# Alternating the heads of the mixer's mix, and conditioning units on Vector and Scalar alone

## The reference

```
def bi_wkv(r, k, v, w, u, time_emb):                   # the conditioning unit; k = v = f, a side input
    tf    = sigmoid(sum(time_emb))
    decay = exp(-exp(w)) * (0.5 + 0.5 * tf)            # one value per (batch, channel)
    ek, ekv = exp(min(k, 30)), exp(min(k, 30)) * v
    nf, df  = forward  scans  a = a * decay + ekv,  b = b * decay + ek
    nb, db  = backward scans of the same
    euk = exp(min(u + k, 30))
    num = nf + nb - ekv + euk * v
    den = df + db - ek  + euk
    return sigmoid(r) * num / max(den, 1e-8) * (0.8 + 0.2 * tf)

x = x + mamba2_mixer(bi_wkv(x, f, f, ...))             # 32 heads of 64, state 128, conv of 4 taps
x = x + moe0(bi_wkv(x, f, f, ...))
x = x + latent_attention(bi_wkv(x, f, f, ...))
x = x + gqa_and_moe1(bi_wkv(x, f, f, ...))
```

## Time and profile before

| | us |
|---|---|
| median of 3 runs | 1410.94 |
| lowest and highest run | 1410.77 to 1413.26 |
| the profiled execution | 1404.55 |
| its span | 1402.80 |
| TensorE busy | 1195.4 (85%) |
| VectorE busy | 850.6 (61%) |
| ScalarE busy | 581.1 (41%) |
| GpSimd busy | 568.0 (40%) |

### The profile page before, as it was taken

How to read it: one execution, slowest core, us unless ns; L and a number is a source line. 1 busy time by engine, 2 the same in 40 slices (tenths; PEclk the granted TensorE clock), 3 DMA queues, 4 the chain that set the end, 5 groups by cost and what they waited for, 6 DMA issues and landing times. The chain is left out here.

```text
span 1402.8 us, 16347 instructions
## 1 busy us (share of the span) xinstructions
PE 1195.4 (85%) x4614; PEld 644.4 (46%) x4614; DVE 850.6 (61%) x1244; ACT 581.1 (41%) x1710; POOL 568.0 (40%) x531
## 2 busy tenths in 40 slices
PE   0059999699995999999968989888898888988998
PEld 0024554355543444444434646443783437844443
DVE  7979996699964752364248749369541695414232
ACT  2025555365542322232226646567571675701110
POOL 5574876248763310020026749357540475400000
PEclk9999999999997999999989999989899898997999
DMA  6000000000034000000030000030000000000000
GB/s 260 0 22 1 1 1 1 1 0 0 0 124 162 0 0 0 0 0 0 34 150 1 1 0 0 17 126 1 1 2 1 1 1 0 1 8 0 0 0 30
DMA packets 5485, 33.28 MB, mean 24 GB/s; under 512 B 528, under 2 KB 1936, under 8 KB 3536
## 3 DMA queue, kind: packets, MB, share of 16 engines
q1 hardware_dynamic: 5424, 32.61, 6.0%
HBM read 31.56 MB, written 1.05 MB: 23 GB/s over the span
## 5 line engine op out<-in xcount | busy, mean ns | idle before, releaser
L806 POOL TENSOR_TENSOR decays<-decays,scores 128x768 f32<-128x768 f32 x64 | 122.6, 1920 | 117.5 <-ACT decays L742 117.2
L575 PE MATMUL pg<-h,weights 128*128 (+1 forms) x136 | 67.5, 621 | 78.0 <-PEq L356 76.7
L1991 POOL TENSOR_TENSOR f_pair<-m,weights 128x256 f32<-128x256 f32 x80 | 91.0, 1156 | 95.4 <-DVE m L2012 94.3
L1094 PE MATMUL ph<-h,weights 128*128 x256 | 115.8, 597 | 0.0
L1399 POOL TENSOR_TENSOR prob_latent<-prob_latent,inverse_latent 128x128 f32<-128x128 f32 (+1 forms) x128 | 81.5, 660 | 70.1 <-DVE inverse_latent L1389 69.7
L742 ACT ACTIVATE decays<-pcum,neg_cum 128x256 f32<-128x256 f32 (+1 forms) x256 | 86.3, 426 | 9.9 <-PE pcum L628 9.6
L1239 DVE TENSOR_TENSOR mid<-up,ph 128x512 f32<-128x512 f32 x44 | 30.2, 687 | 98.5 <-ACT up L1151 98.5
L1399 POOL TENSOR_TENSOR prob_gqa<-prob_gqa,inverse_gqa 128x128 f32<-128x128 f32 (+1 forms) x128 | 62.1, 506 | 58.3 <-DVE inverse_gqa L1389 56.5
L879 DVE SCALAR_TENSOR_TENSOR conv<-px,pp,conv 128x510 f32<-128x510 f32 (+2 forms) x102 | 75.9, 744 | 15.9 <-ACT conv L714 13.5
L1151 ACT ACTIVATE up<-ph 128x512 f32<-128x512 f32 x44 | 26.3, 597 | 140.5 <-PE ph L1094 140.5
L575 PE MATMUL px<-h,weights 128*128 x136 | 70.5, 643 | 14.0 <-DVE conv L879 14.0
(11 more groups left out here) (326 smaller groups left out, 2981.7 us busy)
## 6 DMA issues: line engine op xcount, KB each, us to landing
weights<-in_w_mixer SPq DMA_DIRECT2D x2, 2048.0 KB, 18.4
weights<-in_w_moe SPq DMA_DIRECT2D x2, 1536.0 KB, 8.0
moe_rest<-in_w_moe SPq DMA_DIRECT2D x2, 1536.0 KB, 13.5
weights<-in_w_gqa SPq DMA_DIRECT2D x1, 3072.0 KB, 10.2
weights<-in_w_gqa SPq DMA_DIRECT2D x1, 2048.0 KB, 14.6
weights<-in_w_moe SPq DMA_DIRECT2D x1, 1920.0 KB, 8.7
weights<-in_w_mixer SPq DMA_DIRECT2D x1, 1536.0 KB, 12.6
weights<-in_w_moe SPq DMA_DIRECT2D x1, 1152.0 KB, 12.0
```

Of the source, the lines that this page charges most:

```text
L575: op = nc.tensor.matmul(out[0:m, :], w[:, col + k * m:col + (k + 1) * m], net.h[:, ds(i * PAIR + k * TOK, TOK)], start=(k == 0), stop=(k = ...
L806: nc.gpsimd.tensor_tensor(decays[:, head % 4], decays[:, head % 4], scores[:], ALU.mult).then_inc(decay_scaled, 1)
L1094: op = nc.tensor.matmul(out[:], wt[:, n * D + k * P:n * D + (k + 1) * P], net.h[:, ds(i * PAIR + k * TOK, TOK)], start=(k == 0), stop=(k = ...
L1991: op = nc.gpsimd.tensor_tensor(out[:, :, s, :], src[:, :, 1 - s, :], sin[:, None, s, :].to_broadcast([P, 4, HALF]), ALU.mult)
```

## The change

In `mix`, the loop over the two heads becomes the innermost one: the matmul calls alternate between head 0 and head 1, behind one wait for both heads' decays. The same 16 instructions are issued.

In `CondUnit`, GpSimd's eight operations per unit go. ScalarE gets the four decay spreads (one per channel half and batch entry, a copy of ones with a scale column, 128 x 256) and the copy of e (128 x 1028) as `scalar_operands`; its copy of f goes. VectorE gets e x f, own, own x f, num += num_b and num += ev_pair, two halves each, so that its list has 36 steps and not 26. The waits on GpSimd's semaphores become waits on ScalarE's (`decay_spread`, `e_copied`) and on VectorE's own earlier steps. The operands are issued on ScalarE in the condition stage ahead of each pair's exponential, in the mixer behind the first two convolution starts and ahead of the softplus exponential, in the first MoE stage behind the silu of tile 1, and in latent attention at step 1. The diff, cut:

```diff
-    VECTOR_LINKS = 7 * KT
+    VECTOR_LINKS = 12 * KT + 1
...
-    def pool_operands(self, pair, turn):
...
-    def pool_numerator(self, turn):
...
+    def scalar_operands(self, pair, turn):
         net, nc = self.net, self.net.nc
+        nc.scalar.wait_ge(self.factor_made, turn)
         for kt in range(KT):
+            for b in range(BB):
+                at = (kt * BB + b) * SEG
+                col = net.dcol[:, ds((self.c * KT + kt) * BATCH + pair * BB + b, 1)]
+                nc.scalar.activation(net.decay[:, at + 1:at + SEG],
+                                     net.ones[:, 0:1].to_broadcast([P, SEQ]), ACT.Copy,
+                                     scale=col).then_inc(self.decay_spread, 1)
+        nc.scalar.activation(net.e_pair[:], net.e[:, ds(pair * UNIT, UNIT)], ACT.Copy) \
+            .then_inc(self.e_copied, 1)
+
+    def scalar_exp(self, turn):
         net, nc = self.net, self.net.nc
         nc.scalar.wait_ge(self.u_ready, turn + 1)
         nc.scalar.activation(net.euk[:], net.euk[:], ACT.Exp).then_inc(self.euk_ready, 1)
-        nc.scalar.activation(net.f_pair[:], net.f[:, ds(pair * UNIT, UNIT)], ACT.Copy) \
-            .then_inc(self.f_copied, 1)
...
+        def e_times_f(k):
+            here, both = columns(k)
+            ev_done[k] = link.mark(v.tensor_tensor(net.ev_pair[:, here], net.e[:, both],
+                                                   net.f[:, both], ALU.mult))
...
-                v.wait_ge(self.operand_ready, 4 * turn + operands)
+                v.wait_ge(self.decay_spread, KT * BB * turn + (k + 1) * BB)
+                if x is net.ev_pair:
+                    v.wait_ge(*ev_done[k])
+                if x is net.e_pair:
+                    v.wait_ge(self.e_copied, turn + 1)
...
+        def own(k):
+            here, both = columns(k)
+            v.wait_ge(self.euk_ready, turn + 1)
+            own_done[k] = link.mark(v.tensor_tensor(net.euk[:, here], net.euk[:, here],
+                                                    net.e[:, both], ALU.subtract))
+
+        def own_times_f(k):
+            here, both = columns(k)
+            v.wait_ge(*own_done[k])
+            v.wait_ge(*num_b_done[k])
+            ev_done[k] = link.mark(v.tensor_tensor(net.ev_pair[:, here], net.euk[:, here],
+                                                   net.f[:, both], ALU.mult))
...
         stages = [
-            add_u,
-            scan(net.den, net.e, 2), scan(net.num, net.ev_pair, 3),
-            scan(net.num_b, net.ev_pair, 3, True), scan(net.den_b, net.e_pair, 4, True),
-            combine(net.den, net.den_b), add_own, bound,
+            add_u, e_times_f,
+            scan(net.den, net.e, den_done), scan(net.num, net.ev_pair, num_done), own,
+            scan(net.num_b, net.ev_pair, num_b_done, True),
+            scan(net.den_b, net.e_pair, den_b_done, True),
+            own_times_f,
+            combine(net.num, net.num_b, num_done, num_b_done),
+            combine(net.den, net.den_b, den_done, den_b_done),
+            combine(net.num, net.ev_pair, num_done, ev_done),
+            combine(net.den, net.euk, den_done, own_done), bound,
         ]
...
-                for hh in range(TILE_HEADS):
-                    head = s * TILE_HEADS + hh
-                    pe.wait_ge(decay_scaled, i * HEADS + head + 1)
-                    rows = slice(hh * HEAD, (hh + 1) * HEAD)
-                    for b in range(BB):
-                        for r in range(ST):
-                            cols = slice(0, SEQ) if r == 0 else slice(SEQ, TRI)
+                pe.wait_ge(decay_scaled, i * HEADS + (s + 1) * TILE_HEADS)
+                for b in range(BB):
+                    for r in range(ST):
+                        cols = slice(0, SEQ) if r == 0 else slice(SEQ, TRI)
+                        for hh in range(TILE_HEADS):
+                            head = s * TILE_HEADS + hh
+                            rows = slice(hh * HEAD, (hh + 1) * HEAD)
...
                 begin_conv(i, 1)
+                unit.scalar_operands(i, i + PAIRS)
...
                     if s == 3:
-                        unit.scalar(i, i + PAIRS)
+                        unit.scalar_exp(i + PAIRS)
...
-                unit.pool_operands(i, i + PAIRS)
-                numerator = list(unit.pool_numerator(i + PAIRS))
...
-                    if s in (5, 8, 9, 10):
-                        numerator.pop(0)()
...
+                    if m == 1 and unit:
+                        unit.scalar_operands(i, i + turn0)
                     if m == 2 and unit:
-                        unit.scalar(i, i + turn0)
+                        unit.scalar_exp(i + turn0)
...
+                    if u == 1:
+                        unit.scalar_operands(i, i + 3 * PAIRS)
                     if u == 4:
-                        unit.scalar(i, i + 3 * PAIRS)
+                        unit.scalar_exp(i + 3 * PAIRS)
```

More of the change, by code:

```diff
@@ L249, in columns @@
             return slice(k * n, (k + 1) * n), ds(pair * UNIT + k * n, n)
[L252 to L259, removed]
+        num_done, den_done, ev_done, own_done = ([None] * KT for _ in range(4))
         def add_u(k):
@@ L274, in step @@
                 data = x[:, both if x is net.e else here]
                 order = slice(None, None, -1) if reverse else slice(None)
[L276 to L283, removed]
@@ L284, in scan @@
-            return step
-        def combine(a, b):
+                done[k] = link.mark(v.tensor_tensor_scan(
+                    out[:, here][:, order], net.decay[:, here][:, order],
+                    data[:, order] if reverse else data, 0.0, ALU.mult, ALU.add))
+            return step
+        def own(k):
[3 more added lines that the diff above has]
+                                                    net.e[:, both], ALU.subtract))
@@ L292, in combine @@
-            return step
-        def add_own(k):
-            v.wait_ge(self.own_ready, turn + 1)
-            combine(net.den, net.euk)(k)
+                v.wait_ge(*a_done[k])
+                v.wait_ge(*b_done[k])
+                a_done[k] = link.mark(v.tensor_tensor(a[:, here], a[:, here], b[:, here],
+                                                      ALU.add))
+            return step
         def bound(k):
             here, _ = columns(k)
-            after(k)
-            on(k, v.tensor_scalar(net.den[:, here], net.den[:, here], 1e-8, None, ALU.max))
+            v.wait_ge(*den_done[k])
@@ L303, in invert @@
+            den_done[k] = link.mark(v.tensor_scalar(net.den[:, here], net.den[:, here], 1e-8,
+                                                    None, ALU.max))
         def invert(part):
@@ L305, in invert @@
             if part % (INVERT_PARTS // KT) == 0:
-                after(part * KT // INVERT_PARTS)
+                v.wait_ge(*den_done[part * KT // INVERT_PARTS])
             op = v.reciprocal(net.den[:, cols], net.den[:, cols])
@@ L378, in _ @@
                 .then_inc(pads_ready, 1)
[L380 to L385, removed]
         @block.scalar
@@ L1168, in _ @@
             nc.gpsimd.memset(seg[:, :, 0:1], 0.0).then_inc(zeroed, 1)
-            if unit:
-                with nc.gpsimd.Fori(0, PAIRS) as i:
-                    unit.pool_operands(i, i + turn0)
-                    for step in unit.pool_numerator(i + turn0):
-                        step()
         @block.vector
```

39 lines of the change are left out of this document (15 added, 24 removed).

## The result

The changed kernel takes 1387.03 us (median of 4 runs, 1385.80 to 1387.40) against 1410.86 for the kernel before, a ratio of 0.983 (95% interval 0.981 to 0.984): 23.8 us less, where 28.1 were forecast. Its profiled execution took 1385.80, its span is 1384.0. The changed kernel was timed in this comparison alone; where a later run is set against its 1387.03, two comparisons stand side by side, and the traces say where the difference lies.

The account below looks back on a forecast made before the run. TensorE, busy 85% of the span, was taken as the bound, with VectorE close behind in the mixer. Condition stage 9.2, mixer 15.6 and other stages 3.3 sum to 28.1: median 1410.94 - 28.1 = 1382.8 us, range 1370 to 1397.

Parts of the forecast that it names:

- The condition stage: Condition stage before the mixer: without GpSimd's work a pair takes 28.1 us, two 56.2, gaining 9.2 us.
- The mix: TensorE's mix in the mixer: with heads alternating it shrinks from 2.22 to about 1.5 us.
- B: Rival, mixer: mix stays at 2.2 us, the second head being late for another cause; 1394.0 us, chance 0.12.
- C: Rival, mix: weight loads don't overlap the other head's matmuls, 84 us lost; 1479 us, chance 0.03.
- The full steps: Mixer's twelve full steps: VectorE becomes the bound, 106.1 us in sum, 3.4 us gained per pair.
- rival D: Mixer: VectorE loses both ties of a step to GpSimd, steps become 10.4 us; 1418.0 us, chance 0.04.
- Rival A: Mixer: VectorE's second operation wins its tie against GpSimd, 6.0 us more gained per pair; 1370.8 us, chance 0.13.
- The last steps: Mixer's end: four mixes on the chain each 0.7 us shorter, 2.8 gained per pair, reciprocals hidden in idle time.
- never between: VectorE-GpSimd lock: an added addition in the mixer costs either 0.6 us or the full wait.
- The start of pair 0: Mixer start, first pair: GpSimd's operands no longer hold up cumulative sums, 2.8 less 0.4, so 2.4 us gained.
- That of pair 1: Mixer start, second pair: the same work meets other instructions, a third of the gain taken, 0.8 us.
- Latent attention: Steps before step 12: copy and operands move, GpSimd's numerator collisions go; 1.5 us gained per iteration, 3 for both.

Follow-up runs that it names:

- the second trace: The kernel before, unchanged, run and traced once more: 1410.75 us, with a span of 1408.2.

## Why the prediction was right, and where it was wrong

The time fell inside the range and near the forecast, yet errors of some 12 us to the one side and 8 to the other stand in it. That they nearly cancel is luck: the stages that gave more did so for reasons that the text did not have.

The condition stage, as worked out: 9.06 us for 9.2 forecast in the profiled execution, a pair 28.2 for 28.1. The step that failed was to set this difference off from the median. The execution in the profile had won a tie that the second trace lost, and the text read the 6.4 us between profile and median as if it lay around everything; of the 5.4 between the two traces, all lies in this stage. Only these two executions of the kernel before were traced; 19 of its 31 runs took more than 1409 us, as the second did. Against the second trace the stage gives 14.5.

The mix, as worked out: 1.52 for 1.5, 0.70 saved. Rivals B and C are out (C's loss is 81 us by its own terms, not 84). That weight loads wait for matmuls in flight of the same row group would follow from the Trainium skill (TensorE: Matmul & The Clock Gate, Part 3, "The mechanism"); here a mix with 16 loads and 16 matmuls takes 1.52 us, less than the 2.6 that its matmuls alone would take in line, and its loads are busy for 0.99 of 1.50 us in which matmuls run throughout.

The full steps: the mechanism was right, VectorE paces them at 8.73 and 9.2 with its second piece behind GpSimd's product. The sum was mis-sized by one step: e times f was priced at 8.75 and took 10.96, since there g met the second decay product too and took 2.07 us: two ties lost, as in rival D, but g's and not the first piece's, in one step of twelve. The gain was 2.1 per pair for 3.4. Rival A, that VectorE gets past the tie, did not come by itself but came by moving the pieces, and gave more than its price of 12 us.

The last steps are the step of the sum that failed, for a reason that no rival held. Forecast: four mixes 0.7 shorter, 2.8 gained, in danger only from the reciprocals. Measured: 1.3 and 1.4 us lost from mix 12 to 15, where three of the four mixes should have gained 2.1. The reciprocals are hidden, as said, and cost nothing with full mixes (18.51 in the kernel with the conditioning change alone). Of the 3.4 missing, 2.2 are the step of mix 14: each mix that is shorter moves g against GpSimd's sum of squares, and the longer idle time was then followed by a lower granted clock. The other 1.2 are the step of mix 12, in which TensorE waits for ScalarE's exponentials, since VectorE, the bound until then, brings its taps late. The step of mix 13 gained its 0.70. The idle row 1.66 was read as a constant of the chain, and VectorE's pace was taken to end with the twelve steps. Nor is a loss to GpSimd all or nothing, "never between": g took 0.81, 1.26 or 1.81 us as it started 1.00, 0.55 or 0 us behind GpSimd's sum of 1.26.

The start of pair 0 gave 2.9 for 2.4 (the 0.4 taken off for ScalarE's operands is 0.7 by its own terms, 2.7 less 2.02). That of pair 1 was forecast to gain 0.8 and lost: VectorE's jump back took 2.5 us more, a cost of the longer loop body that the text never considered. Latent attention with the pauses around it gave 3.0 for 3; the first MoE stage 0.3 lost for 0.3 gained. Grouped-query attention was said to stay and gave 2.9, from its own jump back.

In sum: 15.6 forecast for the mixer, 3.5 measured (4.4 against the second trace); the 5.5 that the first trace hid in the condition stage and the 2.9 of an untouched stage made up most of it.

## What to carry to other kernels

A profile is one execution: where two engines start within some tenths of a microsecond of each other and one blocks the other, ask what the stage takes if the tie goes the other way, before its difference is set off from a median. Shortening a matmul group moves everything behind it against other engines, so the last steps of a pipeline must be gone through instruction by instruction, and a wait that has grown can be followed by a lower clock as well. Where VectorE and GpSimd share a step, the order of VectorE's instructions can be worth more than their number: here the same 36 pieces a few instructions earlier gave 23 us.

## What the runs showed of the hardware

A jump back to the start of a loop took VectorE at most 0.3 us in some places and 2.8 to 3.6 in others, with the same body in grouped-query attention (294 entries) in either way; ScalarE's in the mixer took 2.4 to 2.7 in all kernels. TensorE's two column halves, given alternately, run at the rate of one each: 16 matmuls in 1.52 us, with their weight loads beside them. And a granted clock of 0.6 to 0.65 followed idle times of TensorE of 1.9 and 2.8 us at the end of the mixer, while ones of 1.7 to 1.8 left it at 1.00; behind two of 0.66 and 0.85 it fell in three passes over the last steps and stayed at 1.00 in three.
